# Mixture stages: ScalarE issues the write of the gate rows, and SyncE issues the first half's spread ahead of the load and the store

## The reference, cut to what matters

```python
router_probs = jax.nn.softmax(x @ router_w + router_b, axis=-1)      # 8 experts
top_p, top_i = jax.lax.top_k(router_probs, 2)
top_p = top_p / jnp.sum(top_p, axis=-1, keepdims=True)
expert_out = jnp.einsum('bnd,edc->bnec', x, expert_w) + expert_b
gathered = jnp.take_along_axis(expert_out, top_i[..., None], axis=2)
return jnp.einsum('bnk,bnkc->bnc', top_p, gathered)                  # added to t
```

## Time and profile before

| | us |
|---|---|
| median of 3 runs | 6351.87 (6347.93 to 6356.39) |
| the profiled execution | 6351.24 |
| its span in the trace | 6349.4 |
| stage t1, from its first gate save to the last store's landing | 1848 to 2463 |
| stage t3, from its first gate save to the end | 5647 to 6349 |

### The profile page before, as it was taken

The page is one execution under the profiler, slowest core; times in us unless marked ns, Lnnn a source line. Parts: engine busy times, 40 slices in busy tenths (PEclk is TensorE's granted clock), DMA queues, the critical chain, the costliest instruction groups (busy, mean ns, idle before and its releaser), DMA issues. The chain is left out here.

```text
span 6349.4 us, 130784 instructions
## 1 busy us (share of the span) xinstructions
PE 5086.1 (80%) x47166; PEld 3301.8 (52%) x47166; DVE 4350.0 (69%) x9546; ACT 3592.1 (57%) x6867; POOL 1154.7 (18%) x1068
## 2 busy tenths in 40 slices
PE   7887886538968885699969997407999999948887
PEld 4664664224533332599969995104555555523332
DVE  7896887886657777622223446697777777758896
ACT  5775775556545564622243224466766767646775
POOL 2332332052200002400000000131211111121110
PEclk9998998858979997699989999758999999979999
DMA  1111112332348885200000134237666666537877
GB/s 33 38 31 32 38 38 73 77 95 83 108 148 270 278 282 176 79 0 0 0 0 0 54 105 126 69 100 99 81 81 84 83 83 81 68 112 242 247 250 225
DMA packets 745075, 646.30 MB, mean 102 GB/s; under 512 B 496551, under 2 KB 578663, under 8 KB 744627
## 3 DMA queue, kind: packets, MB, share of 16 engines
q1 hardware_dynamic: 743603, 639.06, 40.3%
q0 software_dynamic: 1024, 1.05, 0.1%
HBM read 549.78 MB, written 90.20 MB: 101 GB/s over the span
## 5 line engine op out<-in xcount | busy, mean ns | idle before, releaser
L2420 PE MATMUL sw_pC<-sw_row,sw_wc 128*128 128x128 f32 x10160 | 1158.9, 274 | 56.2 <-DVE sw_row L2295 54.9
L2420 PEld LDWEIGHTS sw_pC<-sw_row,sw_wc 128*128 128x128 f32 x10160 | 1147.6, 191 | 58.2 <-DVE sw_row L2295 55.5
L2854 PE MATMUL sp_pC<-sp_work,sp_bands 64*64 64x512 f32 (+11 forms) x14592 | 986.0, 428 | 44.2 <-issue 44.2
L2283 DVE SCALAR_TENSOR_TENSOR sw_row<-sw_pC,sw_y 128x128 f32<-128x128 f32 x1016 | 337.0, 332 | 792.4 <-PE sw_pC L2420 792.4
L2854 PEld LDWEIGHTS sp_pC<-sp_work,sp_bands 64*64 64x64 f32 x14592 | 601.9, 133 | 431.5 <-issue 365.3
L2793 ACT ACTIVATE sp_pC<-sp_pC,sp_par 128x512 f32<-128x512 f32 x832 | 598.5, 741 | 370.5 <-PE sp_pC L2854 348.0
L1826 DVE TENSOR_TENSOR t_z<-t_z,t_ht 128x1024 f32<-128x1024 f32 x512 | 639.9, 1284 | 100.9 <-DMA t_z<-gate_rows 95.9
L2352 ACT ACTIVATE sw_y<-sw_row 128x128 f32 (+1 forms) x762 | 265.6, 349 | 592.4 <-DVE sw_row L2283 592.4
L1997 PE MATMUL t_pO<-t_z,t_ew 128*64 128x512 f32 x2048 | 519.4, 625 | 95.8 <-DVE t_z L1826 93.4
L2750 DVE TENSOR_TENSOR sp_work<-sp_work,sp_pC 128x512 f32<-128x512 f32 x512 | 351.6, 688 | 170.0 <-ACT sp_pC L2793 169.5
L307 POOL TENSOR_TENSOR wa_sc<-wa_sc,wa_sm 128x1024 f32<-128x1024 f32 x128 | 243.7, 1904 | 677.0 <-DVE wa_sm L396 677.0
(11 more groups left out here) (390 smaller groups left out, 9768.6 us busy)
## 6 DMA issues: line engine op xcount, KB each, us to landing
t_z<-gate_rows SPq DMA_DIRECT2D x512, 512.0 KB, 7.9
sp_bands<-windows SPq DMA_DIRECT2D x128, 512.0 KB
c_spent<-tokens SPq DMA_DIRECT2D x128, 256.0 KB, 2.6
cb_xs<-tokens SPq DMA_DIRECT2D x128, 256.0 KB, 2.8
wa_xs<-in_x SPq DMA_DIRECT2D x64, 256.0 KB, 2.9
tokens<-wa_xt SPq DMA_DIRECT2D x128, 128.0 KB, 1.9
tokens<-cb_h SPq DMA_DIRECT2D x64, 256.0 KB, 2.8
t_xs<-tokens SPq DMA_DIRECT2D x32, 512.0 KB, 11.0
```

The lines of the kernel that those rows point to most:

```text
L2283: dve.scalar_tensor_tensor(row[par][c][:, :, PAD:PAD + P2], pC[c][:, 0:2 * P2].rearrange("p (b w) -> p b w", b=2), 0.0, line(sweep, c, i), ...
L2420: ins = pe.matmul(pC[c][:, 0:2 * P2], wc[:, sweep, m, :], row[1 - par][c][:, :, m:m + P2], start=(m == 0), stop=(m == 4))
L2854: ins = pe.matmul(out[halves[to], :, low * lo:low * hi], band[halves[k], (NV * g + j) % BANDS, q, AT[k][tap], :], v[halves[k], :, low * at ...
```

## The change

ScalarE issues the DMA that writes the gates' rows, directly behind the copy that makes them, after a wait for that copy. SyncE no longer has this issue. In SyncE's loop the spread of half 0 moves ahead of the load and the store (in t3 behind the first `load_columns`); the spread of half 1 stays last.

```diff
-            def keep_gates(m):
-                sp.wait_ge(gs_saved, m + 1)
-                sp.dma_start(gate_rows[m, :, :].rearrange("e (j p) -> (e j) p", p=128),
-                             gs[:, m % 2, :]).then_inc(g_out[m % 2], 16)
-
...
-            keep_gates(0)
             for i in range(2):
                 spread_gates(0, i)
                 if rows is not None:
                     load_columns(7 + i)
             for n in range(NB):
+                if rows is not None and 2 * n + 9 < 2 * NB:
+                    load_columns(2 * n + 9)
+                if n + 1 < NB:
+                    spread_gates(n + 1, 0)
                 if rows is None and XR <= n + 4 < NB:
                     load(n + 4)
-                if rows is not None and 2 * n + 9 < 2 * NB:
-                    load_columns(2 * n + 9)
                 if n > 0:
                     store(n - 1)
-                if n + 1 < NB:
-                    keep_gates(n + 1)
-                    spread_gates(n + 1, 0)
                 if rows is not None and 2 * n + 10 < 2 * NB:
                     load_columns(2 * n + 10)
                 if n + 1 < NB:
...
                 act.activation(gs[:, m.k % 2, :], pT[0][:, 0:128], ACT.Copy).then_inc(gs_saved, 1)
+                act.wait_ge(gs_saved, m.n + 1)
+                act.dma_start(gate_rows.rearrange("m e t -> m (e t)")[bass.ds(m.n, 1), :].rearrange(
+                    "a (k p) -> (a k) p", p=128), gs[:, m.k % 2, :]).then_inc(g_out[m.k % 2], 16)
```

## The result

The changed kernel takes 6391.65 us in the median of 4 runs (6390.45 to 6404.39), the kernel before 6352.06 us (6347.93 to 6356.39). The ratio is 1.0067, 95% interval 1.0049 to 1.0084: slower by 0.7%, where 6390 us was forecast. The profiled execution was the slowest of the four, 6404.39 us (span 6402.6), 12.7 us over their median.

What follows compares the result with a forecast made beforehand. The prediction took a ring through ScalarE and TensorE as the bound, DMAs second. Its terms, 30.8 + 4 + 13 + 8 - 8 - 3 - 6 = +38.8 us on 6351.24 us, gave 6390 us (own range 6372 to 6412; wide range 6342 to 6435).

Steps and rivals of the forecast that it cites:

- The ring: Loop through ScalarE and TensorE that sets the undisturbed beat: 18.37 us in t1, 20.45 us in t3.
- the issue on ScalarE: Behind the gate save in t1 and t3: wait and issue add 0.54 us in 57 beats, +30.8 us (9 to 51).
- The clock: Longer TensorE idle brings more stretches at the lower clock: +4 us in t1, +13 in t3 (bounds 0 and 30).
- Late z in t1: Spreading half 0 first lets gate rows land sooner in t1: -8 us, and -3 in the first beat.
- The y buffer: In t1 the later store nearly ties with the finish needing its buffer: 0.3 us in 28 beats, +8 (0 to 42).
- The image store: In t3's three store beats, half 1 late by 4 us instead of half 0 by 6: -6 us (0 to -18).
- the clock does not care: Rival: t1's lower-clock stretches stay at 12 or 13 and t3 has none; 6373 us, chance 0.14.
- the row is no faster: Rival: the gate row lands no sooner on the second queue, t1's 11 us gain falls out; 6401 us, chance 0.04.
- the y buffer binds: Rival: t1's store lands 1.5 us too late in each of 28 beats, 42 instead of 8; 6424 us, chance 0.14.
- both that rest on a cheap issue: Rivals: issue at 0.3 us a beat, no change, 6351 us (0.15); at 0.16, store beats' 18 us gone, 6331 us (0.13).

Runs made afterwards that it cites:

- e6: The kernel before with ScalarE's wait for its own gate copy alone, SyncE still issuing the gate rows; 6357.9 us (1.0010).
- e8: The changed kernel with SyncE's old order and ScalarE issuing the gate row in its idle time between the two logits copies; 6371.1 us (1.0036).
- e3: The changed kernel with eight unread 128x128 matmuls per beat in TensorE's idle time between the two turns; 6375.8 us (1.0035).
- e4: The kernel before with eight unread 128x128 matmuls per beat between TensorE's two turns; 6362.8 us (1.0015).
- e10: The kernel before with each image store split over eight beats and, in t1, gate rows issued by GpSimd in SyncE's old order; 6320.9 us (0.9954).
- e9: The changed kernel with each image store's eight DMAs issued one per beat over eight beats; 6387.8 us (1.0056).
- e2: The changed kernel with SyncE's old order, ScalarE still issuing the gate rows; 6383.7 us (1.0049).
- e1: The kernel before with SyncE's new order alone, SyncE still issuing the gate rows; 6371.8 us (1.0030).
- e5: The kernel before with SyncE's new order in t1 alone, t3 in the old order, SyncE issuing the gate rows; 6370.7 us (1.0027).
- e11: e10 with SyncE's new order and eight unread filler matmuls per beat in t1; 6319.0 us (0.9948).
- e7: The kernel before with each image store's eight DMAs issued one per beat, the last image as before; 6330.6 us (0.9965).
- e12: e11 with SyncE's old order in t1: GpSimd issues the gate rows, filler matmuls, split image store; 6309.6 us (0.9934).

## Why the prediction was right, step by step

**The ring and the issue on ScalarE: right.** 0.54 us a beat were put on it, 0.56 (t1) and 0.57 (t3) came. The cause is shown by e6 (0.13 for the wait, the rest for the issue) and e8 (no growth when the issue stands in idle time). At 57 beats this is 32 us, for +30.8.

**The clock: right mechanism, far too small in t1.** By 0.04 x 550.79 x 2 and 0.09 x 580.59 x 2, the time at 1.2 GHz went from 44 to some 104 us. The 12 or 13 stretches of the kernel before are confirmed (12 beats below 1.00, one of them twice as far); I had added 5, and 17 came (26 beats, four of them twice as far). Each costs 1.0 us in the longer beat, not 0.8. I had priced the term at +4. The idle of 2.48 us that I took for t1's is that of an undisturbed beat; TensorE's 28 waits there sum to 42.2 us, 1.5 us each. What it was worth depends on which limit is taken out first, because in the kernel before the clock and late z cover each other. With the clock out first (e3 and e4) it was worth 30.5 us in the changed kernel and 1.6 before: +29. With late z out first, what the clock leaves above the ring before is 544.04 - 29 x 18.36 = 11.6 us (e10), which fits the 10 that I had read: +19. By either order +4 was several times too small. For t3 the +13 can't be checked alone in the changed kernel, where late z after the stores lies over it. In e9, without those, 20.5 us stand above the ring at a clock of 0.94.

**Late z in t1: right sign, and the wrong half of the change named.** -8 and -3 were forecast. The first beat gained 22.22 - 19.09 = 3.1 us. Of the 18.1 us over the ring in the 29 beats, I gave 10 to the clock and 8 to late z. With the clock out first, 549.16 - 29 x 18.36 = 16.7 us of late z stay before (e4) and 1.4 in the changed kernel (e3): -15. With late z out first, e10's 11.6 us of clock leave 6.5 of the 18.1 to late z, and in the changed kernel again about 1.4: -5. The forecast of -8 lies between, so its size is not refuted. What removed the late z is the gate row's own queue and the longer beat: e2 has both under the old order, and 5.0 us of z waits. The new order, to which the prediction gave it, works against it (e1, e5, e11).

The prediction also named what speaks against a second issuer. The section "Issuing engines are not separate DMA queues" of the Trainium skill's page "DMA: Bandwidth & Descriptors" says that DMAs of all engines interleave on the same 16 DMA engines, and that starting them on several engines only saves the time of issuing. The measurements decide otherwise for a small write behind large ones. In t1 the 64 KB gate row landed in 6.1 to 8.8 us in the median on SyncE's queue (7.0 before, 6.1 in e7, 8.8 in e1) and in 2.2 to 5.7 us on ScalarE's or GpSimd's (2.2 in the changed kernel, 3.7 in e2, 4.8 in e10, 5.7 in e11). With the order kept, e10 has 16.1 us of z waits where e7 has 51.4.

**The y buffer: wrong by one beat.** +8 were put on it; `finish` never waits for a store. The step that failed is the number of the beat: it set the store of n-1 against a `finish` at T+13.1 that it called `finish(n+1,0)`. In `beat(n)` ScalarE saves the gates of n+1 (that is T) and then finishes n, so the one at T+13.1 is `finish(n,0)`, and it wants the store of n-2, issued a beat before. The trace of the changed kernel shows both sides: with the gate save at 2038.48, `finish(n,0)` starts at 2052.11, T+13.6, and the store of n-1, issued at 2044.08, lands 10.6 us later, at 2054.68 or T+16.2. `finish(n+1,0)`, which needs it, starts at 2072.13:

```profile
2072.13 0.60 ACT L1902 ACTIVATE t_y<-t_pY 128x512 f32<-128x512 f32 x1 [1.45 <-PE t_pY L2002]
```

The store has 2072.13 - 2054.68, some 17.4 us, of slack, and there never was a tie; the landing itself had been counted well enough (T+15.0).

**The image store: wrong sign.** -6 were forecast. The three beats with a store exceed the ring by 28.19 + 29.22 + 30.20 - 3 x 21.02 = 24.6 us, for 18 before: +7. Half 0 is in time now, as forecast, and half 1 is late by more than the 4 us of the count. VectorE's timeline of the first of these beats has it:

```profile
5892.94 1.23 DVE L1819 TENSOR_TENSOR t_z<-t_z,t_ht 128x1024 f32<-128x1024 f32 x1 [7.28 <-DMA t_z<-gate_rows]
```

Counted from the gate save of the beat before, the first part of half 1 landed at T+31.4, 31.3 and 31.0 in the three beats (the same view); the count had T+30.5. But VectorE came to it at T+24.1, 25.2 and 24.1 and not at T+26.5, and waited 7.3, 6.1 and 6.9 us. The lower clock of these beats (0.77 to 0.88, for 0.88 and 0.89 before) is not needed for the excess: in e3, at 0.88, 0.94 and 0.89, they stand 23.9 us above the ring. For the 28 beats of t3 together, 26.4 us were added, of which 28 x 0.57 = 16 are the ring and 10.4 the rest; +7 had been forecast for the rest.

**Sum.** In the profiled execution t1 has -3 for the first beat and 29.8 for the others, of which 16.2 are the ring and 13.6 the clock and late z together (+29 and -15 in the one order, +19 and -5 in the other). Against the forecast, clock and late z of t1 are some +18, the y buffer -8, the rest of t3 +3 and the ring +1: +14 together, and the profiled execution is those 14 us over 6390.

So the median of 6391.65 us was met partly by luck. The two misses of +18 and -8 offset each other in part, and the median lies 13 us below the execution that the terms are read from. Which stretches those 13 us lie in, no trace shows: only one execution was profiled. The mean granted clock on record points at the clock: 0.901 in the profiled execution and 0.904, 0.905 and 0.904 in the other three. At 2 x 0.0033 x 6400 that is some 42 us less at the lower clock, and at the 30.5 us that 104 us of it cost in t1 an estimate gives 12 us. If so, the clock's +29 or +19 is less in a median execution; e3, which takes it away, lies 28 us below the changed kernel by the profiled executions and 16 us by the medians. What was right for its own reason is the ring, at 32 of the 40 us. Of the rivals, e3 refutes that the clock does not care, the landing in 2.2 us that the row is no faster, the trace of `finish` that the y buffer binds, and the 0.56 us both that rest on a cheap issue.

## What to carry to other kernels

Before an issue or a wait is moved to another engine, look whether that engine's instruction lies on the ring that sets the beat: here 0.56 us on a ScalarE that was 57% busy cost 32 us in two stages, before the clock that followed, and on GpSimd, which had nothing to do in t1, an issue of 0.54 us left the ring at 18.36 us (e10). Where two limits lie close together, as the ring, late z and the clock do here, taking one away gives what the next one leaves: the same matmuls were worth 1.6 us in these beats in e4 and 12.3 in e12 (against e10), where late z was gone. The waits of an engine that is not on the ring do not price a limit: 112.8 us of z waits on VectorE went with beats at the ring (e3). A burst of transfers that can wait should not stand ahead of one that can't: eight DMAs issued one in a beat instead of at once gave 22 us (e7).

## What the runs showed of the hardware

- An issue on ScalarE's queue lasts 0.326 us, as on SyncE (0.33), and the next activation starts 0.10 us after it. On GpSimd's the same write's issue takes 0.537 us, and it lands in 4.8 us in the median (tile view of `t_gs` in e10):

```profile
L1772 POOL DMA_DIRECT2D gate_rows<-t_gs x29: 537/537/572, 1866.1 to 2393.9; - x29
...
DMA to landing us min/median/max: 2.7/4.8/5.3
```

- TensorE's idle before the second turn and the lower clock go together, but not beat for beat. In e10 that idle is 71.9 us over the 29 beats of t1, up to 2.5 us each, and some 54 us are spent at 1.2 GHz, in 15 of the 29 beats. In the changed kernel it is 88.4 us, up to 3.1 each, and some 104 us are, in 26 of 29 beats. The beats that stayed at 1.00 have the same idle (3.05 us in the one from 1939.63 and in the one from 2038.48). Eight matmuls that nobody reads, put in that idle, took the 29 beats to 1.00 (e3, e11, e12).
